# Input norm a group ahead, and the small attention products of a unit in one run, in a fused patch-embedding, attention and mixture-of-experts kernel

## The reference

```python
z = _layernorm(patches, ln1_g, ln1_b)
z = jnp.einsum('bnp,pe->bne', z, W_proj) + b_proj
z = _layernorm(z, ln2_g, ln2_b)
h = concatenate([cls, z]) + pos_emb;  h = concatenate([h, txt], axis=1)

x = _layernorm(h)                       # attention, 16 heads of 64
q = jnp.einsum('bsd,hpd->bhsp', x, q_w) + q_b      # k, v alike
scores = jnp.einsum('bhqp,bhkp->bhqk', q, k) / jnp.sqrt(jnp.float32(P))
attn = jax.nn.softmax(scores, axis=2)              # over the queries
ctx = jnp.einsum('bhqk,bhkp->bqhp', attn, v)
h = h + ctx.reshape(...) @ l_w.T + l_b

x = _layernorm(h)                       # 8 experts, top 2, a capacity for each
logits = xt @ w_g
h = h + combine(top2, gelu(x_e @ c_fc[e]) @ c_proj[e])
```

## Time and profile before

| | |
|---|---|
| median of 3 runs | 820.19 us (819.5 to 820.28) |
| profiled execution | 819.61 us, its span 818.0 us |
| granted clock, mean | 0.911 |
| busy: TensorE, weight loads, VectorE, ScalarE, GpSimd | 702.8, 659.7, 524.3, 297.3, 289.0 us |
| first values of g0, first output projection of g1 | 96.0 us, 134.3 us |
| last output projection, first expert matmul | 493.6 us, 541.8 us |

### The profile page before, as it was taken

How to read it: one execution, slowest core, us unless ns; L and a number is a source line. 1 busy time by engine, 2 the same in 40 slices (tenths; PEclk the granted TensorE clock), 3 DMA queues, 4 the chain that set the end, 5 groups by cost and what they waited for, 6 DMA issues and landing times.

```text
span 818.0 us, 17190 instructions
## 1 busy us (share of the span) xinstructions
PE 702.8 (86%) x6444; PEld 659.7 (81%) x6444; DVE 524.3 (64%) x1151; ACT 297.3 (36%) x643; POOL 289.0 (35%) x318
## 2 busy tenths in 40 slices
PE   5366999997979989969799776169999999999996
PEld 5365899896868878968788666069999999999995
DVE  5485477884867867858668783436648567476561
ACT  4242554542523425325245221133324334243240
POOL 4387101012030030120200204452665666657615
PEclk9778999998998989979989956569999999999998
DMA  7631000000000000000000001513543454434412
GB/s 228 195 122 46 1 2 2 23 2 16 23 15 17 8 18 23 2 15 15 15 16 2 22 9 29 180 41 95 114 91 87 80 140 88 96 81 85 83 15 27
DMA packets 52626, 44.31 MB, mean 54 GB/s; under 512 B 25465, under 2 KB 46118, under 8 KB 52562
## 3 DMA queue, kind: packets, MB, share of 16 engines
q1 hardware_dynamic: 23090, 31.51, 12.7%
q0 software_dynamic: 29472, 11.90, 9.2%
HBM read 34.06 MB, written 11.43 MB: 56 GB/s over the span
## 4 chain that ended last, share of the span: by engine, by line
PE 52%; issue 27%; POOL 7%; DMA 6%; DVE 6%; ACT 2%; POOLq 1%; DVEq 0%; ACTq 0%
PE shared L1272 8%; PE shared L1274 7%; PE shared L1273 7%; PE pair L1274 7%; PE pair L1272 7%; PE pair L1273 7%; DMA token_rows<-sent 4%; PE pair L1367 2%; PE ct_ps L1377 2%; PE vt_ps L1354 1%; POOL wq_lo L554 1%; DMA qkv<-patches 1%; PE shared L1413 1%; PE ct_ps L1507 1%; POOL prob L587 1%
## 5 line engine op out<-in xcount | busy, mean ns | idle before, releaser
L727 ACT ACTIVATE qkv<-shared,bq_sb 128x276 f32<-128x276 f32 x192 | 93.7, 488 | 128.9 <-PE shared L1274 128.9
L1272 PE MATMUL shared<-xT_hi,wq_hi 128*128 128x276 f32 x384 | 127.0, 331 | 5.2 <-DVE xT_lo L969 2.4
L681 POOL DMA_INDIRECT out<-yrow,held x48 | 101.4, 2112 | 73.8 <-DVE yrow L1234 60.2
L1273 PE MATMUL shared<-xT_lo,wq_hi 128*128 128x276 f32 x384 | 113.5, 296 | 0.0
L1274 PE MATMUL shared<-xT_hi,wq_lo 128*128 128x276 f32 x384 | 113.3, 295 | 0.0
L837 ACT ACTIVATE act_f<-pair 128x348 f32<-128x348 f32 (+1 forms) x128 | 51.8, 457 | 97.3 <-PE pair L1274 97.3
L1272 PEld LDWEIGHTS shared<-xT_hi,wq_hi 128*128 128x128 f32 x384 | 75.0, 195 | 13.5 <-ACT x2T L765 2.6
L1272 PE MATMUL pair<-xe_hi,fc_hi 128*128 128x348 f32 (+1 forms) x256 | 82.7, 323 | 1.1 <-DVE xe_lo L1216 1.1
L1274 PE MATMUL pair<-xe_hi,fc_lo 128*128 128x348 f32 (+1 forms) x256 | 83.1, 325 | 0.0
L1273 PE MATMUL pair<-xe_lo,fc_hi 128*128 128x348 f32 (+1 forms) x256 | 83.0, 324 | 0.0
L664 POOL DMA_INDIRECT held<-token_rows,found_ix x48 | 67.1, 1399 | 26.8 <-issue 26.8
(11 more groups left out here) (170 smaller groups left out, 1735.3 us busy)
## 6 DMA issues: line engine op xcount, KB each, us to landing
raw_fc<-c_fc SPq DMA_DIRECT2D x8, 1024.0 KB
raw_pj<-c_proj SPq DMA_DIRECT2D x8, 1024.0 KB
qkv<-patches SPq DMA_DIRECT2D x9, 384.0 KB, 4.3
qkv<-w_qkv SPq DMA_DIRECT2D x6, 512.0 KB, 6.2
token_rows<-sent POOLq DMA_DIRECT2D x8, 285.7 KB, 7.2
out<-h SPq DMA_DIRECT2D x8, 276.0 KB
patch_rows<-z_row SPq DMA_DIRECT2D x9, 128.0 KB, 1.7
qkv<-w_l SPq DMA_DIRECT2D x1, 1024.0 KB, 7.1
```

What stands on the lines that cost most here:

```text
L681: pool.indirect_dma_start(out, bass.IndirectOffsetOnAxis(ap=xg[p][0:n, t, D:D + 1].bitcast(U32), axis=0), yrow[p][0:n, t, :], None, bounds ...
L727: act.activation(qkv[(st.i + shift) % 2][:, c, :], shared[bank][:, 0:GT], ACT.Identity, bias=bq_sb[:, c:c + 1]).then_inc(s_free[bank], 1)
L1272: pe.matmul(dst, l_hi, r_hi, start=(first and n == 0), stop=False)
L1273: pe.matmul(dst, l_hi, r_lo, start=False, stop=False)
```

## The change

Four things. On VectorE `norm_in` for group i + 2 moves to u = 1 of group i and `norm_in_end` to u = 4; GpSimd's `root_in` moves behind `add_positions` and also serves group i + 2. `turn_x` of group i + 1 becomes the first thing of u = 0, in one piece, ahead of the output projection, with `bank_uses` to match. On TensorE `context` of unit u moves behind all projections of u, to the start of unit u + 1 behind that unit's special work, so that `context(u - 1)`, `turn_values(u)`, `score(u + 1)` follow each other and all blocks follow them; the last context of a group falls into u = 0 of the next. ScalarE and VectorE follow this order: `put_ctx` and `low_ctx` of u - 1 stand ahead in unit u, ScalarE takes one block ahead of `put_exp` (before: two, in u = 1 three) and the rest behind it, and `weigh_values` is split so that sum and reciprocal (`add_up`) open the unit.

```diff
 def group_uses(g, u):
     uses = []
+    if u == 0 and g + 1 < GROUPS:
+        uses += [("xt", g + 1, c) for c in range(KD)]
     if g >= 1:
         uses += {0: [("proj", g - 1, c) for c in range(KD)],
...
     if g + 1 < GROUPS:
-        if u == 0:
-            uses += [("xt", g + 1, c) for c in range(KD)]
         uses += [("qkv", g + 1, c) for c in qkv_of(u)]
@@ gpsimd
             def stage_b(st):
-                if st.i + 1 < GROUPS:
-                    root_in(st, 1)
                 if st.i + 2 < GROUPS:
                     add_positions(st, 2)
+                    root_in(st, 2)
                 if st.i >= 1:
                     root_mid(st, -1)
                     weigh(st, -1)
...
             add_positions(Step(0), 1)
+            root_in(Step(0), 1)
@@ scalar, in stage_b
                     blocks = list(qkv_of(u)) if more else []
+                    if u == 0 and more:
+                        put_xT(st, 1)
                     if u == 4 and before:
                         put_x2T(st, -1)
-                    ahead = 3 if u == 1 else 2
-                    for c in blocks[:-1][:ahead]:
+                    if u >= 1:
+                        put_ctx(st, u - 1)
+                    elif before:
+                        put_ctx(Step(st.i - 1, st.k, st.span), UNITS - 1)
+                    if u == 0 and before:
+                        put_exp(st, u)
+                        put_y(st, -1)
+                    for c in blocks[:1]:
                         put_qkv(st, 1, c)
-                    if u == 0 and before:
-                        put_y(st, -1)
-                    if u == 0 and more:
-                        put_xT(st, 1)
-                    if u == UNITS - 1:
-                        put_ctx(st, u)
-                    if more or u + 1 < UNITS:
+                    if (more or u + 1 < UNITS) and not (u == 0 and before):
                         put_exp(st, u)
-                    for c in blocks[:-1][ahead:]:
-                        put_qkv(st, 1, c)
-                    if u < UNITS - 1:
-                        put_ctx(st, u)
-                    for c in blocks[-1:]:
+                    for c in blocks[1:]:
                         put_qkv(st, 1, c)
@@ vector
-            def weigh_values(st, u):
+            def add_up(st, u):
                 wait(dve, s_exp, st, lambda i: UNITS * i + u + 1)
                 dve.tensor_reduce(zsum[:, :], expo[u % 2][:, :, :], AX, ALU.add).then_inc(s_zs, 1)
                 wait(dve, s_zs, st, lambda i: UNITS * i + u + 1)
                 dve.reciprocal(zinv[:, :], zsum[:, :]).then_inc(s_zi, 1)
+
+            def weigh_values(st, u):
...
             low_xT(Step(0), 0)
             low_wl(1)
+            norm_in(Step(0), 1)
+            norm_in_end(Step(0), 1)
             take_max(Step(0), 0)
@@ vector, in stage_b
+                    add_up(st, u)
                     if u == 0 and more:
-                        norm_in(st, 1)
+                        low_xT(st, 1)
                     if u == 2 and before:
                         residual(st, -1)
-                    weigh_values(st, u)
-                    if u == 0 and more:
-                        norm_in_end(st, 1)
                     if u == 5 and before:
                         put_logits(st, -1)
+                    if u >= 1:
+                        low_ctx(st, u - 1)
+                    elif before:
+                        low_ctx(Step(st.i - 1, st.k, st.span), UNITS - 1)
+                    weigh_values(st, u)
                     if u == 1 and st.i >= 2:
                         add_table(st, -2)
                     if u == 7 and before:
                         put_place(st, -1)
-                    if u == UNITS - 1:
-                        low_ctx(st, u)
                     if u + 1 < UNITS:
                         take_max(st, u + 1)
...
-                    if u == 0 and more:
-                        low_xT(st, 1)
-                    if u < UNITS - 1:
-                        low_ctx(st, u)
+                    if u == 1 and st.i + 2 < GROUPS:
+                        norm_in(st, 2)
+                    if u == 4 and st.i + 2 < GROUPS:
+                        norm_in_end(st, 2)
@@ tensor, in stage_b
                 for u in range(UNITS):
+                    if u == 0 and more:
+                        turn_x(st, 1)
                     if u == 2 and before:
                         turn_y(st, -1)
-                    turn_values(st, u)
-                    if u + 1 < UNITS:
-                        score(st, u + 1)
-                    elif more:
-                        score(Step(st.i + 1, st.k, st.span), 0)
-                    if u == 0 and before:
-                        project_out(st, -1)
-                    if u == 1 and st.i >= 2:
-                        tabulate(st, -2)
-                    if u == 0 and more:
-                        turn_x(st, 1, range(1))
                     if u == 4 and before:
                         turn_x2(st, -1)
                     if u == 5 and before:
                         logit(st, -1)
                     if u == 7 and before:
                         count(st, -1)
-                    blocks = list(qkv_of(u)) if more else []
-                    for c in blocks[:-1]:
-                        project_qkv(st, 1, c)
-                    context(st, u)
-                    if u == 0 and more:
-                        turn_x(st, 1, range(1, KD))
-                    for c in blocks[-1:]:
+                    if u >= 1:
+                        context(st, u - 1)
+                    elif before:
+                        context(Step(st.i - 1, st.k, st.span), UNITS - 1)
+                    turn_values(st, u)
+                    if u + 1 < UNITS:
+                        score(st, u + 1)
+                    elif more:
+                        score(Step(st.i + 1, st.k, st.span), 0)
+                    if u == 1 and st.i >= 2:
+                        tabulate(st, -2)
+                    if u == 0 and before:
+                        project_out(st, -1)
+                    for c in qkv_of(u) if more else ():
                         project_qkv(st, 1, c)
```

More of the change, by code:

```diff
@@ L802, in _ @@
             sweep(act, stage_b, GROUPS, 2, 2, 2)
+            put_ctx(Step(GROUPS - 1), UNITS - 1)
             put_y(Step(GROUPS), -1)
@@ L1160, in stage_b @@
                         pick(st, -1, 1)
-                    if u == 0 and more:
-                        low_xT(st, 1)
-                    if u < UNITS - 1:
-                        low_ctx(st, u)
+                    if u == 1 and st.i + 2 < GROUPS:
+                        norm_in(st, 2)
+                    if u == 4 and st.i + 2 < GROUPS:
+                        norm_in_end(st, 2)
             sweep(dve, stage_b, GROUPS, 2, 2, 2)
             last = Step(GROUPS)
+            low_ctx(Step(GROUPS - 1), UNITS - 1)
             add_table(last, -2)
@@ L1488, in _ @@
             last = Step(GROUPS)
+            context(Step(GROUPS - 1), UNITS - 1)
             project_out(last, -1)
```

## The result

| | before | after | forecast |
|---|---|---|---|
| median, us | 819.85 (818.91 to 820.28) | 833.0 (831.96 to 834.16) | 831.0 (808 to 842) |
| ratio to before | 1 | 1.0162 [1.0143, 1.0182] | 1.013 |
| profiled execution, its span, us | 819.6, 818.0 | 831.96, 830.3 | |

What follows compares the result with a forecast made beforehand. TensorE was taken to bound the five groups, losing 41 us to idle time and half clock. Group changes -12.5, +2.5, +5.4, +2.6 gave 817.6 profiled; +12.8 for clock and +0.6 for the median gave 831 us, range 808 to 842.

Steps and rivals of the forecast that it cites:

- wait in `turn_x` at five boundaries: Between groups, the second half of `turn_x` waits for the bank of block 23: TensorE idle 3.1 us.
- fourth block of units 1, 3, 5: TensorE waits for ScalarE's second drain before a fourth projection block: 0.4 to 0.55 us, 0.95 in unit 3.
- a group at full clock: Walk of one group from `turn_y`: 51.8 us, 6.8 of them waits, against 54.3 before.
- clock at the boundaries: TensorE's clock falls behind the 3.1 us wait at four of five boundaries, 3.2 us each, 12.8 us.
- up to `turn_y` of g1: First group g0 and g1's own first wait: 2.5 us more than before.
- last `turn_y` to g7's output projection: Units 3 to 7 of g6 take 2.8 us more, the wait for unit 7's `ctx_lo` 2.6: +5.4.
- g7: Last group, without projections: saved copies some 2 us, product held up in units 4, 5, 7 for 4.6: +2.6.
- Rival 1: Clock holds at the boundaries, at most one fall: 817.6 to 821 us, median about 819; chance 0.20.
- rival 4: Clock also falls at g7's wait and fifth boundary, stays low half as long again at three: 839 to 845; chance 0.09.
- The chain at C7: Unit 7, from contexts' start C7: place, maxima, differences, exponentials at +5.90 us, drain at 6.47, bank free at 6.95.
- The small waits: Within groups TensorE waits at fourth blocks, 0.3 us before `turn_x2`, 0.4 before `logit`, 0.5 to 0.6 for `pick`.
- rival 2: Small waits don't come, `turn_x` waits perhaps 1.5 us, groups take 49 to 50: 800 to 812 us; chance 0.14.

Runs made afterwards that it cites:

- e1: Changed kernel, but in unit 7 ScalarE drains both projection blocks ahead of the exponentials; 833.75 us.
- e7: e4 with groups 2 to 5 written out on TensorE only, other engines keeping the loop; 788.25 us.
- e2: e1 plus, at the boundary, ScalarE copying xT and unit 7's contexts ahead of the exponentials and VectorE lowering both ahead of `add_up`; 813.78 us.
- e3: Changed kernel with `put_place`, but for its first two instructions, behind the maxima of the next unit; 823.84 us.
- e4: Kernel before with only the input norm moved ahead (`norm_in`, `norm_in_end`, `root_in` for group i + 2), order of contexts, scores and projections kept; 792.95 us.
- e6: e2 with ScalarE draining two projection blocks ahead of the exponentials in every unit, not in unit 7 only; 798.72 us.
- e9: e6 with groups 2 to 5 written out on TensorE only; 795.48 us.
- e10: e9 with the last group in the order of the kernel before on all engines; 791.53 us.
- e5: Changed kernel with the input norm and `turn_x` put back in unit 0, `turn_x` behind the output projection; contexts, values, scores stay in one run; 846.9 us.
- e11: Changed kernel with groups 2 to 5 written out on TensorE only; 833.48 us.

## Why the prediction was right, point by point

| step of the prediction | forecast | measured |
|---|---|---|
| waits for `xn` from g1 on | gone | gone |
| `xn` itself, in unit 4 | 1.05 | 1.05 |
| wait in `turn_x` at five boundaries | 3.1 | 3.05, 3.08, 2.71 (issue), 3.08, 2.99 |
| fourth block of units 1, 3, 5 | 0.4 to 0.55, 0.95, 0.4 | 0.48, 0.58, 0.24 |
| `turn_x2`, `logit`, `count` | 0.3, 0.4, 0.5 to 0.6 | 0.34, 0.25, 0.34 to 0.42 |
| a group at full clock | 51.8, 6.8 of it waits | 52.5, 5.6 of it waits (e1's one period without a fall) |
| clock at the boundaries | four falls, 12.8 | five, some 10 |
| up to `turn_y` of g1 | +2.5 | +3.5; +5.4 without stage a |
| last `turn_y` to g7's output projection | +5.4, 2.6 of it for `ctx_lo` | +5.5, 2.39 |
| g7 | +2.6 | +3.9, 1.5 of it a fall of the clock |
| sum, profiled | -2.0 + 12.8 = +10.8 | +12.3 |

**The sum, and the luck in it.** The mechanism came as forecast, step by step, but the sum lies nearer to the result than its terms do. The groups at full clock were 3.4 us too short in sum (5 x 0.7), the clock some 3 us too dear, g0 2.9 us too small, and g7's fall of the clock, 1.5 us, was left to the range; in the profile a stage a 2 us shorter took back most of what g0 had too much. These errors happened to cancel.

**The clock.** 27.2 us of the five groups were granted 0.50 (3.4, 6.8, 6.8, 3.4, 6.8), 2.4 of them within the waits themselves, so it costs at most 12.4. What it did cost can be read from periods of the same order without a fall: five times the 52.5 us of e1 are 262.5, 9.7 less than the 272.2 measured; and TensorE is busy for 244.5 us in the five groups against five times 46.9 in e1's period, 10.0. The forecast had 12.8: half of each us at half clock for four falls of 6.4 us. All five boundaries had one, two of them stayed half as long, and a us at half clock cost 0.4 us, not 0.5, as in the kernel before (14.2 us of TensorE's busy time from there to e7, for 34.7 us at half outside the waits). The five groups together took 0.6 us more than before, forecast 0.3. Rival 1 (the clock holds) is out for the changed kernel, but e1 has a wait of 2.75 us after which it held. Of rival 4 two parts came, the fall at the fifth boundary and that at g7 (3.4 us at half behind the wait of 2.39); its third, longer stays at three boundaries, came the other way round.

**The chain at C7,** the heart of the forecast, was right in each link and within 0.15 us. e1, e2 and e3 show that it is this chain: a drain moved alone changes nothing, the order of both engines takes 20 us away, the place behind the maxima 9.

**The small waits** came, against rival 2, though 0.1 to 0.4 shorter than walked. Unit 3's is the largest miss, 0.58 for 0.95. VectorE was late there, as walked, by 0.4 us: with the contexts at 210.68 it could have begun `ctx_lo` at C + 1.19, and began it at 212.25, C + 1.57.

```profile
212.25 0.39 DVE L1005 TENSOR_TENSOR ctx_lo<-ct_ps,ctx_hi 128x276 fp32r<-128x276 f32 x1
```

```profile
215.77 0.39 PE L1278 MATMUL shared<-xT_hi,wq_hi 128*128 128x276 f32 x1 [0.58 <-ACT qkv L727]
```

The bank came at C + 5.09, but TensorE itself asked for it only at C + 4.51 instead of 4.36. So the waits were shorter in part because the work between them was longer, 46.9 us of a period instead of 45.0. The walk had even counted 0.5 us a group as saved by projections in one run. That isn't borne out: in periods at full clock TensorE is busy for 45.8 us in the old order (e4, e7), for 46.9 in the new one (e1, e2, e3) and for 46.0 with two blocks drained ahead (e6, e9). What one block more ahead is worth is e6, 15 us.

**g0 was mis-sized,** by 2.9 us. The wait in unit 1 was in the sum with 2.1 and came with 1.87; but it was followed by half clock for 3.4 us, which no step had, and the first contexts waited another 0.88 us for `vals`:

```profile
103.58 0.39 PE L1278 MATMUL shared<-xT_hi,wq_hi 128*128 128x276 f32 x1 [1.87 <-ACT qkv L727]
```

**g7** came 1.3 us above its +2.6, and that is the clock: without a fall behind the output projection the last group takes 44.5 us in this order (e3, e6, e9), 2.4 more than the 42.1 of before. The three longest waits there are these, at half clock:

```profile
476.62 1.19 PE L1383 MATMUL ct_ps<-expo,vals 69*64 69x69 f32 x16 [2.46 <-DVE vals L998]
...
483.65 1.18 PE L1410 MATMUL shared<-ident,sent 92*128 92x92 f32 x6 [3.65 <-DVE sent L1037]
...
500.48 0.24 PE L1429 MATMUL shared<-chosen_b,tri 92*92 92x16 bf16 x1 [3.79 <-DVE chosen_b L1081]
```

`turn_x2` and `count` wait 3.7 us each for the second norm and for `pick`, and the contexts stand behind them. That they hold up the product was the mechanism named; e10, which puts these two behind, has 43.4 us with a fall of 3.4 in it, near to the 42.1 of before.

**What I had wrong about the kernel before.** Rows 2 and 3 made me write that 41 us are lost to the late norm and its clock, against 46 us a group of real work. Its removal alone brings 27. The clock's share was some 14 by TensorE's busy time (before to e7), not 17, and of the idle time a part was only cover for others: the table in five groups (6.0 us, 1.3 before) and the loop's turn with its fall (4 to 5, e4 to e7). The sum didn't go wrong by this, because it walked the new order unit by unit and didn't subtract the waits from the old time.

**Still open:** why the stay at half clock is 3.4 us after one wait of 3.08 and 6.8 after another of 3.08 in the same execution, and none after e1's 2.75. A wait's length alone doesn't tell it, so a forecast of the clock at such waits is a chance and not a sum.

## What to carry to other kernels

When a dominant wait is taken out, walk the new order unit by unit instead of subtracting the wait: here half a dozen smaller ones, the loop's turn among them, lay under it and came out. Test the parts of a change alone: this one was -27 and +40 us on top of each other, and the slow half was two choices in the order of a draining engine (one block ahead instead of two, and exponentials ahead of the drain that the matmul engine needs), mended with one line and a handful. Even mended, the new order ends 7 us behind the first part alone (e9 and e7), since it gains 3 us in the five groups and loses 9 outside them. A single wait of TensorE of 2.2 to 3.2 us cost mostly 1.4 to 1.8 times its length in this kernel, by the clock behind it, and once only its length; cutting one of 3.1 into two of 1.1 took 9 us off the changed kernel, most of it clock, though its eight executions spread over 8 us.

## What the runs showed of the hardware

- The half clock doesn't set in with the wait's end. Behind the wait that ended at 187.94 contexts and values still take 0.71 and 0.69 us, the scores from 189.59 on 1.21 where they took 0.72 at full clock, and the projection's matmuls are spaced at 0.23 us until 192.9 and at 0.13 from there; the low level is recorded from 189.5 to 192.9. Behind the wait that ended at 241.84 it was there already, from 240.7 to 247.5.
- A wait's length didn't fix the stay at half. Over all profiles, from the first group up to g7's output projection: single waits of 1.04 to 1.68 us were followed by full clock; of thirteen of 1.80 to 1.95 us seven were followed by 3.4 us at half and six by full clock, among these 1.94 with a fall in e2 and 1.94 without one in e6 and e9; waits of 2.23 to 3.18 by 3.4 or 6.8, but e1's 2.75 by full clock; 3.9 to 4.3 (e5) by 3.4 or 6.8, and the 4.2 to 5.9 of before by 6.8 to 10.2. Twice 3.4 us at half stand with no wait above 0.6 us in the 15 us before them (e1 from 443.4, e5 from 287.4), and the matmuls are spaced at 0.23 us there too.
- The turn of TensorE's loop costs 2.2 to 3.2 us of "issue" where nothing lies over it; written out, it is gone, and a period falls from 51.9 to 48.0, the clock's fall included. It was 4.7 us of the median in one version (e4 to e7; 3.8 by the ratios to before, 4.5 between the profiled executions) and nothing in another (after to e11).
- In the profile of e2 the full level of the granted clock stands as 0.95, while equal matmuls are spaced at 0.127 us as in all others. A mean clock is only to be compared with the level of its own profile.
